# A two-layer decoder on one core: the maxima of eight heads share one transposed tile, and scores by key start four steps later

## The reference

```python
x = _layernorm(x + _L0_attn_ref(x, ...))          # 16 heads, rotary positions, biases
x = _layernorm(x + _L0_xattn_ref(x, ctx, ctx, ...))  # 16 heads, keys and values from ctx
x = _layernorm(x + _L0_ffn_ref(x, ...))           # 8 experts of 512, two chosen per token
x = _layernorm(x + _L1_attn_ref(x, ...))          # one head, causal
x = _layernorm(x + _L1_xattn_ref(x, ctx, ctx, ...))  # 16 heads again
x = _layernorm(x + _L1_ffn_ref(x, ...))           # 8 experts, one per token, 128 slots each
# inside a 16-head attention
score = jnp.einsum('bhqd,bhkd->bhqk', Q, K) / jnp.sqrt(8)
out = jnp.einsum('bhqk,bhkd->bhqd', jax.nn.softmax(score, axis=-1), V)
```

## Time and profile before

| | us |
|---|---|
| median of 3 runs | 463.71 |
| lowest and highest | 457.6 and 465.71 |
| the profiled execution | 460.74 |
| its span in the trace | 458.9 |
| PE busy | 389.6 (85%) |
| PEld busy | 332.9 (73%) |
| DVE busy | 282.9 (62%) |
| ACT busy | 245.0 (53%) |

### The profile page before, as it was taken

The page is one execution under the profiler, slowest core; times in us unless marked ns, Lnnn a source line. Parts: engine busy times, 40 slices in busy tenths (PEclk is TensorE's granted clock), DMA queues, the critical chain, the costliest instruction groups (busy, mean ns, idle before and its releaser), DMA issues.

```text
span 458.9 us, 9054 instructions
## 1 busy us (share of the span) xinstructions
PE 389.6 (85%) x3284; PEld 332.9 (73%) x3284; DVE 282.9 (62%) x829; ACT 245.0 (53%) x551; POOL 48.5 (11%) x57
## 2 busy tenths in 40 slices
PE   2589799999889999999988999989999779784292
PEld 1477577777679888788977899868989566653292
DVE  2487787878864637545287545574655885844544
ACT  2226366766576565466637665566565556451141
POOL 6202900000000000000000000000000101020115
PEclk9989899999999999999999999999999999896597
DMA  7606120612200200001101000200020003550300
GB/s 269 186 23 176 34 69 7 199 36 63 46 2 1 47 3 0 1 2 25 23 1 41 8 1 1 46 1 1 2 46 2 13 1 101 166 171 0 102 13 31
DMA packets 18907, 22.53 MB, mean 49 GB/s; under 512 B 2984, under 2 KB 13361, under 8 KB 18864
## 3 DMA queue, kind: packets, MB, share of 16 engines
q1 hardware_dynamic: 17344, 18.68, 14.8%
q10 hardware_dynamic: 1008, 2.31, 1.5%
q0 software_dynamic: 512, 0.97, 0.6%
HBM read 13.63 MB, written 2.11 MB: 34 GB/s over the span
## 4 chain that ended last, share of the span: by engine, by line
PE 74%; DVE 13%; issue 6%; ACT 2%; DMA 1%; POOL 0%; POOLq 0%; DVEq 0%; ACTq 0%
PE bank_D L821 13%; PE bank_D L672 10%; PE bank_C L698 9%; PE bank_A L683 9%; PE bank_A L809 4%; DVE negmax L1183 3%; PE bank_A L811 3%; PE bank_A L810 3%; PE bank_A L613 3%; PE bank_K L593 3%; PE bank_A L614 2%; PE bank_D L658 2%; PE bank_D L727 2%; PE bank_A L1475 2%; PE bank_A L737 1%
## 5 line engine op out<-in xcount | busy, mean ns | idle before, releaser
L1183 DVE TENSOR_REDUCE negmax<-bank_D 128x2 f32<-128x512 f32 x192 | 128.3, 685 | 45.6 <-PE bank_D L672 44.8
L957 ACT ACTIVATE expo<-bank_A 128x512 f32<-128x512 f32 x192 | 111.6, 598 | 59.6 <-PE bank_A L683 57.7
L672 PE MATMUL bank_D<-k_head,q_sp 128*128 128x256 f32 x384 | 90.9, 322 | 0.6 <-DVE negmax L1183 0.4
L683 PE MATMUL bank_A<-q_sp,k_head 128*128 128x256 f32 x384 | 80.9, 296 | 0.1
L993 ACT ACTIVATE hidden<-bank_A,b 128x256 f32<-128x256 f32 x128 | 53.8, 473 | 44.0 <-PE bank_D L821 29.3
L672 PEld LDWEIGHTS bank_D<-k_head,q_sp 128*128 128x128 f32 x384 | 59.7, 195 | 14.7 <-issue 10.7
L821 PE MATMUL bank_D<-mix_w,hidden 128*128 128x128 f32 x512 | 67.7, 275 | 0.2 <-DVE ctx_n L1110 0.2
L821 PEld LDWEIGHTS bank_D<-mix_w,hidden 128*128 128x128 f32 x512 | 62.3, 191 | 0.8 <-issue 0.8
L1240 DVE SCALAR_TENSOR_TENSOR y_mixture<-bank_D,g_w,y_mixture 128x128 f32<-128x128 f32 x64 | 22.4, 350 | 64.1 <-PE bank_D L821 64.1
L683 PEld LDWEIGHTS bank_A<-q_sp,k_head 128*128 128x128 f32 x384 | 59.6, 193 | 1.9 <-issue 0.8
L698 PE MATMUL bank_C<-expo,v_aug 128*32 128x256 f32 x768 | 51.4, 385 | 1.2 <-ACT expo L957 1.2
(11 more groups left out here) (180 smaller groups left out, 530.1 us busy)
## 6 DMA issues: line engine op xcount, KB each, us to landing
k_head<-k_sp SPq DMA_DIRECT2D x96, 64.0 KB, 2.0
mix_w<-in_mix_w SPq DMA_DIRECT2D x24, 256.0 KB, 3.7
expo<-in_mix_w SPq DMA_DIRECT2D x6, 256.0 KB, 3.8
proj_w<-in_proj ACTq DMA_DIRECT2D x1, 640.0 KB, 11.5
xe_scratch<-empty_row SPq DMA_DIRECT2D x1, 520.0 KB, 4.3
expo<-xe_scratch SPq DMA_DIRECT2D x2, 260.0 KB, 3.1
expo<-in_spread SPq DMA_DIRECT2D x1, 512.0 KB, 8.2
expo<-in_spread ACTq DMA_DIRECT2D x1, 512.0 KB, 8.5
```

The costliest lines, as they stand in the source:

```text
L672: last = mm(where(seq, b, ("max", k))[:, qt * SEQ:(qt + 1) * SEQ], q_sps[SET[seq, b]][:, k // 4, qt * P:(qt + 1) * P], k_heads[SET[seq, b] ...
L683: last = mm(where(seq, b, ("exp", h))[:, kt * SEQ:(kt + 1) * SEQ], k_heads[SET[seq, b]][:, t, g, kt * P:(kt + 1) * P], q_sps[SET[seq, b]][ ...
L957: activate(expos[SET[seq, b]][:, h % ESLOTS, :], where(seq, b, ("exp", h))[:], ACT.Exp, scale=float(HD) ** -0.5).then_inc(free(seq, b, ("e ...
L1183: V.tensor_reduce(negmaxes[SET[seq, b]][:, s // 4, :, 32 * (s % 4)], where(seq, b, ("max", s))[:].rearrange("p (q n) -> p q n", q=QT), AX. ...
```

## The change

Instead of four groups of four heads, the maxima are handled in two pairs of groups. A pair's eight maxima lie in one `negmax` tile: head g of the even group in row 32g, of the odd group in row 32g + 1. One shift transposes both (two matmuls instead of four), and DVE adds the transposed tile to both groups' `q_sp` at once, by a broadcast operand. So that each head picks its own row, the keys of odd groups are one in row 32g + 1 (`C_KODD`); for this the copy of the spread keys on ACT is split into one instruction for each group, four per attention instead of two, 48 in the kernel instead of 24.

A pair is complete only after eight maxima: shifts stand at steps 9 and 17, scores by key begin at 11 instead of 7, and all later steps of an attention are moved by four. The projection of the values moves from step -7 to -3. The tables of starts are moved: the last attention starts at tick 195 instead of 188, and the list ends 11 ticks later. The last weights use the smaller `negmax` and a `ctx_sb` buffer.

```diff
-SHIFT_AT = 5
-EXP_AT = 7
-VALUES_AT = 12
-BACK_AT, CTX_AT, OUT_AT, ROOT_AT, NORM_AT, TURN_AT = 25, 26, 27, 28, 29, 30
+OWN_VALUES_AT = -3
+SHIFT_AT = 9
+EXP_AT = 11
+VALUES_AT = 16
+BACK_AT, CTX_AT, OUT_AT, ROOT_AT, NORM_AT, TURN_AT = 29, 30, 31, 32, 33, 34
...
 ATTENTION = [(0, SELF0, 0), (1, SELF0, 16), (2, SELF0, 32), (0, CROSS0, 48), (1, CROSS0, 64),
-             (3, SELF0, 80), (2, CROSS0, 96), (3, CROSS0, 117), (0, CROSS1, 133), (1, CROSS1, 149),
-             (2, CROSS1, 167), (3, CROSS1, 188)]
-MIXTURE = [(0, MIX0, 79), (1, MIX0, 99), (2, MIX0, 127), (3, MIX0, 148)]
+             (3, SELF0, 80), (2, CROSS0, 96), (3, CROSS0, 121), (0, CROSS1, 137), (1, CROSS1, 153),
+             (2, CROSS1, 171), (3, CROSS1, 195)]
+MIXTURE = [(0, MIX0, 83), (1, MIX0, 103), (2, MIX0, 131), (3, MIX0, 156)]
...
+def pair_at(step, start):
+
+    pair, rest = divmod(step - start, 8)
+    return pair if rest == 0 and 0 <= pair < 2 else None
...
-        negmaxes = sets("negmax", [P, GROUPS, QT, P])
+        negmaxes = sets("negmax", [P, 2, QT, P])
...
-                def shift(seq, b, t):
+                def shift(seq, b, pair):
                     pe.wait_ge(ld_const, 16)
-                    wait_drained(pe, seq, b, ("max", 4 * t + 3))
-                    wait_free(pe, seq, b, ("shift", t))
+                    wait_drained(pe, seq, b, ("max", 8 * pair + 7))
+                    wait_free(pe, seq, b, ("shift", pair))
...
-                        activate(k_sp[:, 2 * half:2 * half + 2, :],
-                                 where(seq, b, f"sk{half}")[:].rearrange("p (t n) -> p t n", t=2),
-                                 ACT.Identity, bias=const[:, C_KONE:C_KONE + 1]
-                                 ).then_inc(free(seq, b, f"sk{half}"), 1)
+                        for odd, one in enumerate((C_KONE, C_KODD)):
+                            last = activate(k_sp[:, 2 * half + odd, :],
+                                            where(seq, b, f"sk{half}")[:, odd * SEQ:(odd + 1) * SEQ],
+                                            ACT.Identity, bias=const[:, one:one + 1])
+                        last.then_inc(free(seq, b, f"sk{half}"), 1)
...
-                            V.tensor_tensor(q_sp[:, t, :], q_sp[:, t, :].bitcast(f32),
-                                            where(seq, b, ("shift", t))[:, 0:SEQ], ALU.add
-                                            ).then_inc(free(seq, b, ("shift", t)), 1)
+                            V.tensor_tensor(q_two, q_two.bitcast(f32),
+                                            where(seq, b, ("shift", pair))[:, 0:SEQ].unsqueeze(1)
+                                            .broadcast_to([P, 2, SEQ]), ALU.add
+                                            ).then_inc(free(seq, b, ("shift", pair)), 1)
```

More of the change, by code:

```diff
@@ L165, in attention @@
                 turn(seq, b, "xT", "A")
-            if group_at(s, SHIFT_AT) is not None:
-                turn(seq, b, ("shift", group_at(s, SHIFT_AT)), "D")
+            if pair_at(s, SHIFT_AT) is not None:
+                turn(seq, b, ("shift", pair_at(s, SHIFT_AT)), "D")
             if 0 <= s < HEADS:
@@ L234, in constants @@
     c[0::32, C_KONE] = 1.0
+    c[1::32, C_KODD] = 1.0
     c[:, C_EPS] = EPS
@@ L578, in _ @@
                         if what[1] == 0:
-                            last, block_before = ATTENTION[-2][:2]
-                            sp.wait_ge(group_done[last], GROUPS * (MHA[block_before] + 1))
+                            wait_filled(sp, *ATTENTION[-2][:2], "back")
                         e = what[1] // 2
@@ L759, in attention @@
                             transpose_x(seq, b)
-                        if group_at(s, SHIFT_AT) is not None:
-                            shift(seq, b, group_at(s, SHIFT_AT))
+                        if pair_at(s, SHIFT_AT) is not None:
+                            shift(seq, b, pair_at(s, SHIFT_AT))
                         if 0 <= s < HEADS:
```

40 lines of the change are left out of this document (21 added, 19 removed).

## The result

Measured side by side, the kernel before took 461.01 us (median of 4, 457.60 to 465.71) and the changed kernel 469.00 us (median of 4, 468.25 to 470.29). Some executions of one and the same program run at a lower granted clock and take longer (the 465.71 above), and ratios leave them out. The ratio is 1.0212 with a 95% interval of 1.0172 to 1.0253: slower beyond doubt, though the interval does not settle whether by more than 2%. The forecast of 459.7 us, a slight gain, had the wrong sign; 469.0 lies at the upper end of its range. The profiled execution of the changed kernel took 468.25 us, its span 466.4.

What follows compares the result with a forecast made beforehand. PE, busy for 85% of the span, was taken as the bound. Terms -4.6 - 0.8 - 1.9 - 0.8 + 0.3 + 0.8 + 1.6 + 4.4 gave -1.0 on 460.74: 459.7 us, range 448 to 470.

Steps and rivals of the forecast that it cites:

- Scores by key four steps later: Ticks with maxima or scores alone cost +0.8 before first scores, +1.6 at (3, CROSS0), +4.4 at the end; work otherwise same.
- second sign of being wrong: The forecast would be wrong if the clock row showed new low slices near 235 or 390 us.
- the waits go with the crowd: Faster rival, chance 0.20: the tail leaves the keys' spread ticks, so PE's other waits shrink too; -13.0, 447.7 us.
- Shifts on PE: 24 of 48 shifts go, 19 counted at 0.24 us of PE each: -4.6 us, bounds 3.1 and 5.8.
- Values and tails: Values' three ordinary waits for the division go, -1.9; the long one loses -0.8, its stall beside POOL stays.
- Key copies on ACT: 24 key copies of 0.685 us become 48 of 0.480; PE feels +0.3 us, bounds 0 and 3.5.
- The SP queue: Key copies wait for an earlier attention's last score; 4.5 us needed, six ticks taking 5.3 at hand: cost 0.
- The end: Last gap and one more group of scores with its product (2.93 us) behind the last maximum: +4.4 us.
- The longer list costs whole ticks: Slower rival, chance 0.10: each of 11 added ticks costs 1.74 us, +19.1 in all; net +13.7, 474.4 us.
- late key copies: Rival, chance 0.03: PE stands before six first maxima waiting for key copies, 1 us each; 465.7 us.
- covered transposes: Rival, chance 0.14: weight loads or bank order set the pace, so removing shifts gains nothing on PE; 464.3 us.
- first sign of being wrong: The forecast would be wrong if PE's waits outside the end fell by more than 5 us in total.

Runs made afterwards that it cites:

- e6: The kernel before with only the values' projection moved, to step -3 instead of -7; 455.1 us, ratio 0.9922.
- e9: e6 with the changed kernel's longer list of starting ticks and nothing else; 463.0 us, ratio 1.0084.
- e11: e9 with the tail at steps 29 to 34 instead of 25 to 30; 471.1 us, ratio 1.0265.
- e2: The kernel before with every table and step of the change, but four shifts and whole key copies; 482.7 us, ratio 1.038.
- e3: The changed kernel with whole key copies, two activations of 512 an attention as before; 468.3 us, ratio 1.0174.
- e14: e6 with the queries' spread at step -2, behind the transposed result, instead of -3; 463.1 us, ratio 1.0078.
- e7: e5 with the queries' spread at step -1 instead of -3; 465.3 us, ratio 1.0136.
- e8: e5 with the transposed result at step 35 instead of 34, mixtures and the starts behind them one later; 463.4 us, ratio 1.0087.
- e12: The changed kernel with the maxima matmuls of the last attention's first twelve heads written three times; 470.9 us, ratio 1.0244.
- e4: The kernel before without the shifts and additions of groups 1 and 3, that part of the computation missing; 450.5 us, ratio 0.9767.
- e5: The changed kernel with the spread of the keys at step -6 instead of -7; 462.8 us, ratio 1.0075.
- e10: e6 with the spread of the keys at step -6 instead of -7; 459.7 us, ratio 1.0012.

## Why the prediction was wrong

The chain of experiments gives each step a measured size (us of 460, each uncertain by 2 to 5), and the steady stretch a second one:

| step | kernels | forecast | measured | in the steady stretch |
|---|---|---|---|---|
| values to -3 | before to e6 | -2.7 | -3.6 | -0.86 |
| longer list | e6 to e9 | +3.7 | +7.5 | +0.01 |
| tail four steps later | e9 to e11 | 0 | +8.3 | +1.22 |
| exponentials, scores by key, products four later | e11 to e2 | +3.1 | +5.3 | +0.42 |
| pairs: half the shifts, longer additions | e2 to e3 | -5.4 | -9.5 | -0.65 |
| key copies in halves | e3 to changed | +0.3 | +1.7 | +0.28 |
| sum | | -1.0 | +9.7 (9.8 measured at once) | +0.42 |

The forecast's +6.8 for thin ticks is split here: the gap at (3, CROSS0) and the three ticks of the last gap (1.6 + 1.2 + 0.9) come with the longer list, the ticks before the first scores and the very end (0.8 + 2.3) with the later scores.

- **The step that failed is "Scores by key four steps later".** It said "the work is the same" and came to +6.8 us; e6 to e2 measured +21.1. Two things are wrong in it. First, it gave no price at all to every attention's tail standing beside other steps of its neighbours: +8.3 us. The attentions start 16 ticks apart, so steps 25 to 30 stood beside -7 to -2 of the one two later, eight and eight spread matmuls and their projections, which PE worked through while DVE and ACT carried the tail. Steps 29 to 34 stand beside -3 to 2. e9 and e11 show it with the tail alone, e14 with the cover alone; e7 and e8 set the limit of this reading, as shorter waits did not pay there. Second, the thin ticks that it did price were priced at about half: 3.7 against 7.5 for the list, where PE's added time is busy time at a lower clock and not idle time, and 3.1 against 5.3 for the later scores, a figure that by itself is hardly clear of its error of 4.4. For that one there was no experiment of its own, but the traces of e11 and e2 show two places: from the last maximum to `back` it is 6.8 and 10.8 us, and the stretch from the third attention's first maximum to the fourth's takes 20.2 and 23.1: in e2, as in the changed kernel, the norm meets POOL's weight split there (2.29 us of wait instead of 1.29) and the clock falls behind it.
- **The second sign of being wrong came true.** The prediction wanted no new low slices in the clock row near 235 or 390 us. Slice 21 (233 to 245 us) went from 9 to 8 and slice 35 from 8 (390 to 402) to 6 (396 to 408). The mean granted clock fell from 0.961 to 0.944, which is about 52 us at half clock instead of 36, an estimate from these two means. What that costs is not settled. At the end e12 lifted it without gain. At 301 to 308 us it can be read: from the first maximum of (1, CROSS1) to that of (2, CROSS1) the changed kernel takes 48.8 us with that stretch at half clock, e3 and e12 take 46.7 and 46.8 without it.
- **The rival "the waits go with the crowd" had the mechanism with the wrong sign.** It took the crowd for what delays the tail; the crowd is what PE does while it waits. The row that spoke for it, the waits of L737 in the earlier trace rows, did not say what stood ahead in PE's order at the places without a long wait; the timeline of such a tick would have, and I read only the ticks with a wait.
- **Shifts on PE: right sign, half the size.** I took the shift and the pair right behind it, 0.24 us. The whole cycle without one is 0.41 shorter, and pairing gave 9.5 us with the additions, against 5.4. The changed additions came out at 0.680 us (0.70 estimated).
- **Values and tails.** The ordinary waits went entirely and the long one with them (5.3 to 0), more than the 1.9 forecast; but the stall beside POOL stayed, as forecast, and moved on to the spread. That POOL would meet a norm as well (62.19 us, above) was not foreseen; the upper bound named the queries' split. The changed kernel's timeline:

```profile
47.80 0.72 DVE L1107 TENSOR_TENSOR rope<-rope 128x256 f32<-128x256 f32 x1
...
49.07 1.26 POOL L507 TENSOR_TENSOR w_lo<-mix_w,w_hi 128x512 fp32r<-128x512 f32 x1
49.17 1.44 DVE L1109 TENSOR_TENSOR qk_lo<-rope,qk_hi 128x256 fp32r<-128x256 f32 x1
...
50.71 0.36 PE L620 MATMUL bank_A<-qk_hi,spread 128*128 128x256 f32 x1 [2.87 <-issue]
```

  The subtraction again takes 1.44 us beside POOL's, as in the earlier trace rows, and the 3.40 us in front of the values are 2.87 in front of the spread. By the rule that the prediction quoted from the Trainium skill ("SBUF — State Buffer", section "SBUF: two separate sides") the stall goes only with the overlap; the trace agrees, as both stayed.
- **Key copies on ACT: right.** 48 rows of 0.478 us (0.480 taken), and e3 tells them hardly from nothing (1.7 us with an error of 3.3; 0.28 us in the steady stretch). **The SP queue: right.** No maximum waits for `k_head` in the changed kernel, and a landing takes 2.0 us as in the earlier trace rows.
- **The end: right sign, too small.** From the end of the last maximum to `back` it is 412.26 - 405.89 = 6.4 us before and 419.31 - 408.16 = 11.2 after, 4.8 more, where 2.93 was priced. The changed kernel was at half clock for the first part of it (0.50 granted up to 408 us, 0.66 from 408 to 412).
- **"The longer list costs whole ticks"**, the slower rival at 0.10, came nearest as a difference (+13.7 against +9.8), by luck: its ticks cost 0.7 us, not 1.74, and the rest of what it filled in was the lost cover and the end. That the time of 469.0 lies inside the stated range is luck of the same kind, since the range reached up there for late key copies and covered transposes, and neither happened. That the transposes were covered fell with e4.

The prediction's first sign of being wrong, PE's waits changing by over 5 us outside the end, was set only downwards; they rose.

## What to carry to other kernels

On an engine that runs in a written order, before moving a step look at what stands between it and the step of the other engine that it waits for, and at what it itself covers for its neighbours. "Same work, other tick" is free only if both stay filled, and a tick is never moved alone: it takes its partners' cover with it. Work covers only from the right place, behind what the other engine does first (e7 against e14). Look also at what a third engine does at the new time, as POOL at the norm here. Try the parts of such a change separately; here the smallest one, the values at -3, beats both kernels (0.9922), and what was bundled with it hid that.

## What the runs showed that I had not expected

- A transposing pair of fp32 128x128 costs a stream of matmuls 0.41 us, three times the 0.13 us from its start to that of the next pair (3.52 us a cycle with it, 3.11 without); the rest is three slower pairs behind it, 0.1 each.
- A DVE step over 128x2 numbers, 0.16 us elsewhere, took 1.15 beside POOL's subtraction (62.19 us). With the half clock that followed, one such meeting lengthened 16 ticks from 20.3 to 23.2 us.
- Eleven more ticks cost 7.5 us without a microsecond of idle time on PE (65.8 in e6 and in e9): the same matmuls were busy for 8.6 us more, at a lower clock.
- PE at half clock for ten microseconds near the end (0.56 and 0.50 granted, 400 to 408 us), could be lifted to 0.95 to 1.00 by repeated matmuls, and the end came no earlier: DVE is busy for 3.6 to 3.7 of 4 us there.
- Eight matmuls moved by one tick went with -6.3 us (e5, most of it at the place where the norm no longer met POOL), +4.1 (e10, the same edit in another layout) and +7.2 (e14).
